# Normalised rows stored as 16-bit halves and turned by the load, in place of a TensorE turn, in a two-layer cross-attention kernel

## The reference

```python
x = x + xattn0(layernorm(x), ctx)     # 16 heads of 64, softmax over 77 keys
x = x + ffn0(layernorm(x))            # silu(gate) * up, then down; hidden 768
x = x + xattn1(layernorm(x), ctx)     # the rows that the change touches
x = x + ffn1(layernorm(x))            # int8-quantised 256x256 product
```

## Time and profile before

| what | value |
|---|---|
| median of 3 runs | 1629.7 us (1627.35 to 1631.89) |
| the profiled execution's own time | 1632.44 us |
| its span | 1630.6 us |
| granted TensorE clock, mean | 0.994 of full |
| PE busy | 1568.4 us, 96% of the span |
| weight loads (PEld) | 1420.3 us, 87% |
| ACT busy | 1379.6 us, 85% |
| DVE busy | 1358.4 us, 83% |
| POOL busy | 1270.9 us, 78% |
| DMA traffic | 305.79 MB, mean 188 GB/s; hardware queue 82.1% of 16 engines' span |

### The profile page before, as it was taken

The page is one execution under the profiler, slowest core; times in us unless marked ns, Lnnn a source line. Parts: engine busy times, 40 slices in busy tenths (PEclk is TensorE's granted clock), DMA queues, the critical chain, the costliest instruction groups (busy, mean ns, idle before and its releaser), DMA issues.

```text
span 1630.6 us, 70351 instructions
## 1 busy us (share of the span) xinstructions
PE 1568.4 (96%) x25178; PEld 1420.3 (87%) x25178; DVE 1358.4 (83%) x3519; ACT 1379.6 (85%) x5665; POOL 1270.9 (78%) x1892
## 2 busy tenths in 40 slices
PE   7999978999999999999999999999999999999995
PEld 4655668999999999999999999989999999999994
DVE  5777767888888888888888887888899899989885
ACT  5665677889998998998898888888999999999993
POOL 3300058898998988988988988778999999999984
PEclk9999999999999999999999999999999999999998
DMA  8975679897787787787787988889899889989995
GB/s 239 324 281 226 223 183 170 169 176 174 172 175 178 165 179 176 166 180 172 166 181 171 176 168 160 151 173 193 190 200 199 190 190 200 199 189 190 197 182 107
DMA packets 732248, 305.79 MB, mean 188 GB/s; under 512 B 621424, under 2 KB 717584, under 8 KB 730064
## 3 DMA queue, kind: packets, MB, share of 16 engines
q1 hardware_dynamic: 730272, 297.29, 82.1%
q0 software_dynamic: 1840, 6.82, 1.3%
HBM read 87.72 MB, written 65.54 MB: 94 GB/s over the span
## 4 chain that ended last, share of the span: by engine, by line
PE 35%; POOL 30%; issue 12%; DVE 5%; DMA 3%; ACT 1%; POOLq 0%; SPq 0%; ACTq 0%; DVEq 0%
PE psum L301 24%; POOL pr L1481 10%; POOL p L1488 8%; POOL p L1484 6%; PE psum L1110 4%; PE psum L299 4%; POOL hT_l L1471 3%; POOL rs L361 2%; DMA pT<-p 2%; PE psum L1126 2%; PE psum L292 1%; DVE oT_l L330 1%; DVE x L1460 1%; POOL y L1509 1%; DMA x2T<-x 1%
## 5 line engine op out<-in xcount | busy, mean ns | idle before, releaser
L1225 ACT ACTIVATE ex<-psum,nmax 128x77 f32<-128x77 f32 x2048 | 638.0, 335 | 46.2 <-DVE nmax L1342 37.1
L1225 ACT ACTIVATION_READ_ACCUMULATOR ex<-psum,nmax 128x1 f32 x2048 | 443.1, 216 | 0.0
L1488 POOL TENSOR_TENSOR p<-pr,p 128x308 f16<-128x308 f32 x512 | 413.1, 807 | 38.4
L1481 POOL TENSOR_TENSOR pr<-ex,rden 128x308 f32<-128x308 f32 x512 | 369.1, 721 | 63.7 <-DVE rden L1347 63.1
L301 PE MATMUL psum<-xT,wq_h 128*64 128x256 f16 x3552 | 304.5, 273 | 0.0
L1342 DVE TENSOR_REDUCE nmax<-psum 128x4 f32<-128x308 f32 x512 | 241.2, 471 | 63.6 <-PE psum L301 53.7
L1484 POOL CAST p<-pr 128x308 f16<-128x308 f32 x512 | 241.7, 472 | 43.0 <-DMA pT<-p 10.7
L301 PE MATMUL psum<-xT,wq_l 128*64 128x256 f16 x1776 | 245.9, 273 | 0.0
L301 PE MATMUL psum<-kb,qT_h 128*64 128x154 f16 x3584 | 228.0, 231 | 11.1 <-DVE qT_l L333 6.9
L301 PE MATMUL psum<-wo_h,oT_h 128*64 128x256 f16 x1536 | 214.2, 275 | 12.2 <-DVE oT_l L330 11.2
L1110 PE MATMUL psum<-pT,vb 77*64 77x256 f16 x3072 | 213.0, 274 | 0.6 <-DMA pT<-p 0.6
(11 more groups left out here) (167 smaller groups left out, 3805.4 us busy)
## 6 DMA issues: line engine op xcount, KB each, us to landing
keys<-ks SPq DMA_DIRECT2D x16, 1232.0 KB, 5.3
kb<-keys SPq DMA_DIRECT2D x256, 77.0 KB, 2.6
vb<-vals SPq DMA_DIRECT2D x128, 154.0 KB
vals<-vs SPq DMA_DIRECT2D x64, 256.0 KB, 3.1
x_pair<-in_x_dram SPq DMA_DIRECT2D x32, 256.0 KB, 3.1
pT<-p SPq DMA_TRANSPOSE x512, 3.3
x_res<-in_x_dram SPq DMA_DIRECT2D x32, 256.0 KB, 3.0
mid_x<-y SPq DMA_DIRECT2D x32, 256.0 KB, 2.4
```

The costliest lines, as they stand in the source:

```text
L1225: last = act.activation(ex[i][:, t, b, :], SC[:, t, b * NK:(b + 1) * NK], ACT.Exp, bias=nmax[i][:, t, b:b + 1], accum_out=den[i][:, t, b:b ...
L1481: pool.tensor_tensor(pr[:, t, :, :], ex[i][:, t, :, :], r, ALU.mult).then_inc(s_p, 1)
L1488: pool.tensor_tensor(d[:, t, 1, :, 0:NK], pr[:, t, :, :], d[:, t, 0, :, 0:NK], ALU.subtract).then_inc(s_pl, 1)
```

## The change

The layer-0 output rows are split into halves as soon as they are normalised: ACT writes the high half of `y16` at the end of u = 3, DVE the low half in u = 0 of the next step, between `hidden(4)` and the reciprocals. SP stores `y16` (128 partitions of 2 KB, the same number of bytes as before) in u = 1 of that next step. In layer 1, SP's load of `xn` becomes a DMA transpose from that store straight into `xT`; it waits for the store and for the last queries that read the same `xT` buffer. TensorE's four transposes, ACT's high half and DVE's low half in u = 1 are gone, as are their PSUM bank use and semaphores.

```diff
--- before.py
+++ after.py
@@ -89,7 +89,7 @@
         mid_d = nc.dram_tensor("mid_x", (B, NQ, D), F32).ap()
-        nrm_d = nc.dram_tensor("mid_n", (B, NQ, D), F32).ap()
+        nrm_d = nc.dram_tensor("mid_n", (B, P, QT * 2 * D), F16).ap()
@@ -829,6 +829,7 @@
         yn = sb("yn", [P, QT, D], F32)
+        y16 = sb("y16", [P, QT, 2, D], F16)
         x2 = sb("x2", [P, QT, D], F32)
@@ -851,7 +852,6 @@
         s_xr, s_xb, s_x1 = sem("s_xr"), sem("s_xb"), sem("s_x1")
-        s_nl = sem("s_nl")
         s_s, s_m, s_e, s_r = sem("s_s"), sem("s_m"), sem("s_e"), sem("s_r")
@@ -863,18 +863,18 @@
         s_y, s_ys = sem("s_y"), sem("s_ys")
+        s_y16h, s_y16l = sem("s_y16h"), sem("s_y16l")
         s_am, s_ls, s_li, s_qa, s_qi = sem("s_am"), sem("s_ls"), sem("s_li"), sem("s_qa"), sem("s_qi")
...
         out_rows = out.rearrange("b (t p) d -> b p t d", p=P)
-        n_rows = nrm_d.rearrange("b (t p) d -> b p t d", p=P)
...
-        FAR = range(-3, 4)
+        FAR = range(-4, 4)
@@ -892,8 +892,6 @@
                 if u == 1:
-                    if lay[1] == 1:
-                        out.append(("turned_x", 0))
                     if lay[-2] == 0:
@@ -1001,6 +999,8 @@
                         b_mid = h - 3
+                    if lay[-4] == 0:
+                        b_nrm = h - 4
                     if lay[-2] == 1:
@@ -1037,16 +1037,18 @@
                             load_values(1, at_own, lay[0])
-                        if u == 3 and lay[-3] == 0:
-                            sp.wait_ge(s_yn, QT * (h - 2))
-                            sp.dma_start(batch_of(n_rows, b_mid), yn[:, :, :]).then_inc(s_ys, 16)
+                        if u == 1 and lay[-4] == 0:
+                            sp.wait_ge(s_y16l, h - 3)
+                            sp.dma_start(nrm_d[bass.ds(b_nrm, 1)].rearrange("o p c -> (o p) c"),
+                                         y16[:, :, :, :].rearrange("p t r d -> p (t r d)")).then_inc(s_ys, 16)
                         if turning:
...
                             sp.wait_ge(s_ys, 16 * (h + 4 - B))
-                            after(sp, s_x16l, B - 1 if h + 2 == B else 0)
-                            after(sp, s_xt, h + 3 - B)
-                            sp.dma_start(xn, batch_of(n_rows, b_far)).then_inc(s_nl, 16)
+                            sp.wait_ge(s_q, UNITS * (h + 1))
+                            sp.dma_start_transpose(xT[like % 2][:, :, :, :, :].rearrange("p t r k q -> p (t r k) q"),
+                                                   nrm_d[bass.ds(b_far, 1)].rearrange("o p c -> (o p) c")).then_inc(
+                                                       s_xd, 16)
                         if u == 3 and lay[3] == 0:
@@ -1157,10 +1159,8 @@
                         if ("q", u) in plan:
-                            if u == 2 and lay[1] == 0:
+                            if u == 2:
                                 pe.wait_ge(s_xd, 16 * (h + 1))
-                            if u == 2 and lay[1] == 1:
-                                pe.wait_ge(s_xl, h + 3 - B)
                             queries(pe, (u + 2) % UNITS, lay[(u + 2) // UNITS], (like + (u + 2) // UNITS) % 2, bank("q", u), paired(u, lay))
@@ -1170,9 +1170,6 @@
                             gate_up(5, bank("gu", 5))
-                        if u == 1 and lay[1] == 1:
-                            pe.wait_ge(s_nl, 16 * (h + 2 - B))
-                            turn(pe, bank("turned_x", 0), xn).then_inc(s_xt, 1)
                         if u == 2 and lay[-3] == 0:
@@ -1255,10 +1252,6 @@
                             high(act, qT_h[(u + 1) % 2][:, :, :], RG[(u + 1) % 2], Q_DOWN).then_inc(s_qh, 1)
-                        if u == 1 and lay[1] == 1:
-                            act.wait_ge(s_xt, h + 3 - B)
-                            high(act, turned_rows((like + 1) % 2, 0),
-                                 bank("turned_x", 0).rearrange("p k (t q) -> p t k q", q=P)).then_inc(s_xh, 1)
                         if u == 1 and lay[-3] == 0:
@@ -1282,7 +1275,7 @@
                             act.wait_ge(s_nmr[2], h - 2)
-                            act.wait_ge(s_ys, 16 * (h - 2))
+                            after(act, s_y16l, h - 3)
                             normalise(act, yn, y, rs3, 2, s_yn)
@@ -1292,6 +1285,10 @@
                             high_hidden(2, h - 2)
+                        if u == 3 and lay[-3] == 0:
+                            act.wait_ge(s_yn, QT * (h - 2))
+                            act.wait_ge(s_ys, 16 * (h - 2))
+                            high(act, y16[:, :, 0, :], yn[:, :, :]).then_inc(s_y16h, 1)
@@ -1412,11 +1409,6 @@
                                                          op1=ALU.mult).then_inc(s_ya, 1)
-                        if u == 1 and lay[1] == 1:
-                            dve.wait_ge(s_xh, h + 3 - B)
-                            low(dve, turned_rows((like + 1) % 2, 1),
-                                bank("turned_x", 0).rearrange("p k (t q) -> p t k q", q=P),
-                                turned_rows((like + 1) % 2, 0)).then_inc(s_xl, 1)
                         if u == 1 and lay[-1] == 1:
@@ -1430,6 +1422,9 @@
                             hidden(4, h - 3)
+                        if u == 0 and lay[-4] == 0:
+                            dve.wait_ge(s_y16h, h - 3)
+                            low(dve, y16[:, :, 1, :], yn[:, :, :], y16[:, :, 0, :]).then_inc(s_y16l, 1)
                         if u == 3 and lay[-2] == 0:
```

## The result

| | before | after |
|---|---|---|
| median of 4 runs each, in turns on one chip | 1630.8 us | 1653.74 us |
| lowest to highest | 1627.35 to 1632.49 | 1653.17 to 1656.16 |
| span of the profiled execution | 1630.6 us | 1651.4 us |

A forecast was written before the change was run, and what follows sets the result against it. The prediction took TensorE's work plus its short stalls as the bound. It summed +14.6 and +0.9 for layer 0 and -9.9 for layer 1 to +5.6 us, from a median of 1629.7 to 1635.3, range 1619 to 1648.

The forecast's parts named there:

- What bounds the kernel: Both layers: time is the sum of TensorE's work and its short stalls; other engines cost only where TensorE waits.
- The layer-0 term, 27 x 0.54 = 14.6: Layer 0, u = 0: the new DVE subtraction queues with POOL, delaying `gate_up(0)` 0.54 us a step over h = 4 to 30.
- PE can't win it back: Layer 0: the 0.54 us a step stays lost, since DVE's way to the next `x216` starts anew from PE.
- The delay of `oT_l`: Layer 0, next unit: `oT_l` comes later on DVE, but its delay overlaps with `gate_up(0)`'s and the larger counts.
- ACT's high half, cost 0: Layer 0, end of u = 3: at most 0.63 us, of which ACT's wait for `nmr` hides 0.44; cost 0.
- The store in u = 1, cost 0: Layer 0, SP: the moved store delays a probability turn by under 0.6 us, its reader two units away; cost 0.
- Layer 1, 29 x 0.34 = -9.9: Layer 1, end of u = 1: without TensorE's turn `project` starts 0.34 us earlier a step, h = 34 to 62.
- What is late next: Layer 1: POOL, waiting 0.42 us a step for DVE's `ve`; the gain could not go past 0.42.
- Steps h = 31 to 33, +0.9: Last layer-0 steps: the turn's removal and the new wait leave about +0.3 us each.
- Rival A: Layer 0: the new subtraction fits in, costing 0 to +3 us over 30 steps; about 1620 us, faster; chance 0.25.
- Rival D: Layer 0 pays less than half, +0.2 us a step, as POOL is later in phase; 1626 us; chance 0.1.
- Rival C: Layer 1, SP and DMA: the transpose makes keys or probability turns late; 1645 us at 0.34 a step; chance 0.2.

The follow-up runs named there:

- nmr_later: The changed kernel with DVE's `nmr` of the next input rows moved behind `oT_l` in u = 2; 1647.55 us, 1.0109.
- no_low: The changed kernel without DVE's low half of `y16`, all waits kept; 1625.99 us, 0.9970.
- low_first: The changed kernel with DVE's low half of `y16` one place earlier, ahead of `hidden(4)` in u = 0; 1628.52 us, 0.9990.
- no_y16: The changed kernel without DVE's low half and without ACT's high half of `y16`; 1626.79 us, 0.9977.
- halves: The changed kernel with DVE's low half of `y16` cut into two 128x256 instructions in u = 2, store moved to u = 3; 1642.11 us, 1.0061.
- low_psum: low_first with the subtraction's first operand read from PSUM instead of SBUF; 1628.38 us, 0.9989.
- halves_db: halves with two `y16` buffers, ACT waiting for the store before last; 1628.8 us, 0.9983.
- low_stats: The changed kernel with DVE's low half of `y16` replaced at its place by two `bn_stats` of `yn`, one SBUF operand each; 1629.86 us, 0.9993.
- low_u2: The changed kernel with DVE's low half of `y16` moved to u = 2 ahead of `out_rows(0)`, and its store to u = 2; 1633.73 us, 1.0019.

## Why the prediction was wrong

- **What bounds the kernel** held. No engine became a bound, and all that layer 0 lost is in PE's short stalls.
- **The layer-0 term, 27 x 0.54 = 14.6, is the step that failed.** It measured 25.1, by the starts of `gate_up(0)` (1.1 us ahead of before in h = 3, 24.0 behind in h = 30). Its mechanism was right: DVE and POOL take turns, the order that the earlier trace rows gave came true instruction by instruction, and u = 0 costs 0.41 and 0.61 against the two steps before, for the 0.45 and 0.63 that were forecast (mean 0.51 for 0.54). What failed is the sentence on "PE can't win it back", which ended the count there: it assumed that u = 0 is the only place hurt. In u = 2 `nmr` falls behind POOL instead of ahead of it (0.71 for 0.18), which costs `down(1)` another 0.46 (nmr_later: 0.54 a step less in the profiled execution when cured). That it falls behind because the delay of u = 0 has shifted DVE against POOL is read from the timelines; no_low and low_first, where u = 0 is not late, have no such steady wait. I had two steps of the trace and looked at only one unit of each.
- **The delay of `oT_l`** was said to overlap with that of `gate_up(0)`, the larger counting. So it did: +0.26 there, +0.51 in all.
- **ACT's high half, cost 0**: right (no_y16 is no faster than no_low). **The store in u = 1, cost 0**: right as far as no_low shows. It isn't free at any place: in halves, with the store in u = 3, ACT waited for it in the last steps of layer 0.
- **Layer 1, 29 x 0.34 = -9.9**, is the second term that was mis-sized: it came to -2.8, in a steady step to -0.19. At the place itself the term was right (-0.33; 0.06 us of hand-over). Lost was 0.11 a step, since `yo` changed places with POOL's cast, and only some 21 of the 29 steps were steady ones. POOL's wait for `ve` did not vanish either: from 1100 to 1550 us it is 5.9 us in 21 waits, 0.28 each, for 9.8 in 23, 0.43 each. "What is late next" was asked of one wait of POOL and not of the exclusion that had carried layer 0. The first steps of the layer take another 1.0 back; what makes them longer is open.
- **Steps h = 31 to 33, +0.9**: by the starts of `gate_up(0)` they gained 0.6 us instead, for a reason that was not looked for.
- **Rival A** (it fits in) did not happen as the change stands; it is what happens one place earlier, in low_first, and there the gain of layer 1 is left: 1628.5, against its 1620. **Rival D**, 0.2 us a step, fell with the 0.96. **Rival C**, SP and DMA in layer 1, did not happen. The issue of the transpose takes 1.285 us and it lands in 3.5, and the share of the DMA engines rose from 0.89 to 0.96, but from 1100 to 1550 us PE's waits for DMAs are only 0.9 us for keys (0.5 before) and 0.9 for probabilities (none before). The Trainium skill (Advanced Engine Details and Errata, "X-Bar Transpose (TRN2)") has transpose DMAs as fast as regular ones; here the issue of the same 256 KB took 1.285 us for 0.531, but on the total the rule's conclusion held.
- **The range** ended at 1648. The far end that the text named for layer 0, 1.0 us a step, gives just that by itself: 27.0 + 0.9 - 9.9 = +18.0. With the measured 2.8 for layer 1 it gives +25.1, 1654.8. The two ends were never combined, though one mechanism, the exclusion of DVE and POOL, stood behind both.

## What to carry to other kernels

Before a DVE instruction with two SBUF operands is added, lay the whole step of DVE and POOL side by side, not only the unit of the edit: for each such instruction, even one of 128x2, see whether it comes ahead of or behind POOL's, by how many hundredths, and who waits behind each. Try the new instruction one place up and one place down: here one place decided 25 us, more than the whole change could gain. Where DVE's record begins less than 0.03 us behind POOL's, the starts don't tell which engine will pay, and only a run does. An operand that can be read from PSUM takes the instruction out of this queue (low_psum). With low_first (1628.52) or halves_db (1628.8) the change is 0.1 to 0.2% under the kernel before, which can hardly be told from it (intervals up to 1.0000 and 0.9993).

## What the runs showed of the hardware

The Trainium skill (SBUF — State Buffer, "Who interferes with whom") says that a DVE instruction with two SBUF inputs and a GpSimd instruction that reads SBUF exclude each other, and that whoever is first holds the port for its whole length; one SBUF input does not contend, unless the instruction runs in a two-port mode, as `tensor_scalar` can. The runs agree: the subtraction took 0.68 or 0.95 by who came first, low_psum, with one operand in PSUM, left POOL's record at 0.75 where low_first made it 1.30, and low_stats, with one SBUF operand, took 0.74 in two instructions and left the step at 24.83. An exception shows too: `ve`, a `tensor_scalar` of 128x2 with one SBUF operand, takes 0.17 us, but up to 0.51 in low_first where POOL's L1483 is at work; in which mode it ran, no run shows. What I had not expected:

- An instruction of 128x2 elements pays as much as one of 128x512: this `nmr` took 0.71 for 0.18, 0.53 more, where the subtractions took 0.27 to 0.54 more. Over all of them from 325 to 922 us the mean is 0.493 us before (72) and 0.486 after (70): not more was paid, but by another of them, one with PE behind it.
- Who is first is decided by a few hundredths of a us. In all twelve traces, from 325 to 1550 us, the two-operand instructions of DVE whose record began at most 0.12 us away from one of POOL's waited each time if POOL's began 0.03 us or more ahead (1113 records), and none waited that began ahead itself (363). In between the starts don't tell: 0.01 to 0.02 us behind POOL's L1483 DVE went first (low_first, 24 steps), as far behind POOL's cast it waited (`yo`).
- Records on both sides hold the wait inside them as busy time, so no view of idle time shows it. Only a record's length against its fastest sibling does.
- The state is stable: in the changed kernel 22 steps in a row take 25.77 to 25.78, where before they alternated between 24.3 and 25.3, and they alternate again in no_low, low_u2 and halves_db but not in low_first. This kernel falls into one phase or another, and a small edit chooses it.
